# Perceiver and delta-rule block: inverses in whole lines, Gram halves by ScalarE with masks on GpSimd, new lists of turns

## The reference

```
x = x + xattn(layernorm(x), ctx)        # causal self-attention, attention over 257 context rows, FFN 128-512-128
x = x + attn(layernorm(x))              # two layers of a delta rule with 8 heads, each followed by a gated FFN of 352
x = x + ffn(layernorm(x))               # 32 experts of 64, top 8 within the best 4 of 8 groups, one shared expert
```

```
def step(S, inps):
    qi, ki, vi, bi = inps
    pred = jnp.einsum('bhkv,bhk->bhv', S, ki)
    S = S + bi[..., None, None] * ki[..., :, None] * (vi - pred)[..., None, :]
    o = jnp.einsum('bhkv,bhk->bhv', S, qi)
```

## Time and profile before

| what | value |
|---|---|
| median of three runs | 730.24 us (728.17 to 730.74) |
| the profiled execution | 727.0 us, of which the span is 725.2 |
| TensorE busy | 582.2 us, 80% |
| VectorE busy | 446.4 us, 62% |
| ScalarE busy | 269.7 us, 37% |
| GpSimd busy | 105.2 us, 15% |
| mean granted TensorE clock | 0.834 of full |

### The profile page before, as it was taken

One profiled execution on the slowest core, in us unless ns is written; L12 is line 12 of the kernel. 1 busy time (PEld: TensorE's weight loads), 2 busy tenths in 40 slices (PEclk: granted clock), 3 DMA queues, 4 the chain that ended last, 5 costly groups with the idle time before them and its releaser, 6 DMA issues.

```text
span 725.2 us, 15630 instructions
## 1 busy us (share of the span) xinstructions
PE 582.2 (80%) x6608; PEld 387.7 (53%) x6608; DVE 446.4 (62%) x1103; ACT 269.7 (37%) x571; POOL 105.2 (15%) x148
## 2 busy tenths in 40 slices
PE   2787970877598899787589768996688999999994
PEld 1543650466497867655388635873453444444442
DVE  4856495879947244937845881676666555555553
ACT  1465530554622634354544345234332222222221
POOL 2545372420000102110200010111200000000000
PEclk9888995775557599889657977898979999999998
DMA  9995013000000000000000220000122634334321
GB/s 343 309 368 208 1 23 95 0 2 3 1 3 4 1 3 2 2 1 2 0 2 4 85 103 2 3 3 1 34 61 64 147 87 118 100 101 117 87 59 29
DMA packets 19077, 46.68 MB, mean 64 GB/s; under 512 B 3808, under 2 KB 8544, under 8 KB 18752
## 3 DMA queue, kind: packets, MB, share of 16 engines
q1 hardware_dynamic: 18368, 45.43, 20.7%
q10 hardware_dynamic: 640, 0.26, 0.2%
HBM read 43.32 MB, written 2.36 MB: 63 GB/s over the span
## 4 chain that ended last, share of the span: by engine, by line
PE 60%; DVE 21%; ACT 9%; POOL 3%; SPq 2%; issue 2%; DMA 1%; DVEq 0%; POOLq 0%
PE psum L736 8%; PE psum L731 8%; PE psum L741 7%; PE psum L579 5%; ACT arena L759 4%; PE psum L606 4%; PE psum L668 3%; PE psum L694 3%; PE psum L565 3%; PE psum L697 3%; PE psum L703 2%; PE psum L657 2%; PE psum L647 2%; POOL rstd L939 2%; SPq L413 2%
## 5 line engine op out<-in xcount | busy, mean ns | idle before, releaser
L918 ACT ACTIVATE arena<-psum 128x512 f32<-128x512 f32 x68 | 40.6, 597 | 131.9 <-PE psum L731 124.0
L1358 DVE TENSOR_TENSOR arena<-psum,arena 128x512 f32<-128x512 f32 x64 | 44.3, 692 | 62.5 <-PE psum L736 60.7
L741 PE MATMUL psum<-arena,wed_sb 128*128 128x512 f32 x128 | 66.2, 599 | 0.0
L759 ACT ACTIVATE arena<-psum 128x512 f32<-128x512 f32 (+1 forms) x72 | 34.3, 503 | 63.9 <-PE psum L565 38.1
L565 PE MATMUL psum<-arena 32*64 32x128 f32 x1024 | 44.1, 331 | 11.5 <-DVE XA L1275 6.8
L1363 DVE TENSOR_TENSOR arena<-arena 128x512 f32<-128x512 f32 x64 | 44.3, 692 | 13.6 <-PE psum L741 13.6
L565 PEld LDWEIGHTS psum<-arena 32*64 32x64 f32 x1024 | 38.0, 167 | 17.9 <-DVE XA L1275 7.8
L938 POOL TENSOR_TENSOR ve<-ss,eps_rms 128x4 f32<-128x4 f32 x16 | 4.5, 282 | 291.9 <-ACT yr L810 208.1
L469 PE MATMUL psum<-ident,yn 128*128 128x128 f32 x72 | 15.9, 379 | 38.3 <-DVE yn L1024 21.3
L741 PEld LDWEIGHTS psum<-arena,wed_sb 128*128 128x128 f32 x128 | 24.9, 194 | 31.7 <-issue 24.0
L579 PE MATMUL psum<-wed_sb,arena 64*64 64x32 f32 x512 | 28.2, 291 | 14.7 <-ACT arena L759 14.7
(11 more groups left out here) (285 smaller groups left out, 1225.1 us busy)
## 6 DMA issues: line engine op xcount, KB each, us to landing
arena<-shares SPq DMA_DIRECT2D x64, 256.0 KB, 4.0
arena<-in_ctx_t SPq DMA_DIRECT2D x16, 514.0 KB, 8.6
arena<-in_ctx_z SPq DMA_DIRECT2D x16, 512.0 KB, 9.8
XA<-in_x SPq DMA_DIRECT2D x1, 1024.0 KB, 4.8
zlast<-in_ctx_last SPq DMA_DIRECT2D x4, 256.0 KB, 17.4
X<-x_mid SPq DMA_DIRECT2D x2, 512.0 KB, 4.4
weg_sb<-in_we_gate SPq DMA_DIRECT2D x2, 512.0 KB, 6.3
weu_sb<-in_we_up SPq DMA_DIRECT2D x2, 512.0 KB, 7.1
```

The lines of the kernel that those rows point to most:

```text
L741: pe.matmul(x3, wed_sb[:, (p - 1) % (NPAIR + 1), :], act_a[pr], start=(p == 0), stop=False, skip_group_check=True).then_inc(x_down[pr], 1)
L759: return act.activation(out_, in_, ACT.Copy, scale=scale)
L918: act.activation(act_g[pr], banks[4 * pr + 2 * (n % 2)], ACT.Silu).then_inc(x_silu[pr], 1)
L1358: dve.tensor_tensor(act_gu[pr], banks[4 * pr + 1], act_g[pr], ALU.mult).then_inc(x_gu[pr], 1)
```

## The change

There are four edits.

1. The transposed inverses are written to `back` with the 16 rows of a block side by side: `(n r)` in place of `(r n)`. VectorE's transpose back (L1306 after) so writes with a stride of 16 words, and the spread on ScalarE reads 16 words side by side.
2. ScalarE copies both halves of a Gram quarter, the key half to GA and the query half to BD, and signals after the second. TensorE's next quarter waits for that signal. The VectorE step is gone.
3. GpSimd multiplies each quarter of BD by the triangle in place, and signals `g_diag`; the "o" step on TensorE waits for the four of them.
4. Both lists of turns are other ones.

```diff
-XTURNS = "AABAABABBABAAAAAABABABABAABABBAABBBABBBABABBBB"
+XTURNS = "ABABAABBAABAAAAAABABABAABAABABBAABBBBBBABABBBB"
...
-TURNS = ("AABAABAABAABBAABABABAABBAABAABABBAABAABBAAAAAAABBABABAABBABABAABABABAABAABABABBBABABABABAABAABAB"
+TURNS = ("AAAABABABAABBBBBAAAAAABABABAABBABBAABABBABBAAAABAAAABBAABBABAAAAABBABAAAAAABBAAABABBAABAABBBABABB"
...
                         if q == 0:
                             pe.wait_ge(k_bq, i + 1)
                         else:
-                            pe.wait_ge(g_diag[u], pi * 4 + q)
+                            pe.wait_ge(g_a[u], pi * 4 + q)
...
                     elif kind == "o":
                         pe.wait_ge(s_u[u], pi * 3 + 3)
+                        pe.wait_ge(g_diag[u], pi * 4 + 4)
...
-                        copy(quarter(GA[g], q), gram_part(bank, 0)).then_inc(g_a[u], 1)
+                        copy(quarter(GA[g], q), gram_part(bank, 0))
+                        copy(quarter(BD[g], q), gram_part(bank, 1)).then_inc(g_a[u], 1)
...
-                        lanes = back[pr].rearrange("p (r n) -> p n r", r=C16)[:, u * NB:(u + 1) * NB, :]
+                        lanes = back[pr].rearrange("p (n r) -> p n r", r=C16)[:, u * NB:(u + 1) * NB, :]
...
+                    elif kind[:4] == "gram":
+                        q = int(kind[4])
+                        pool.wait_ge(g_a[u], (l * 2 + pr) * 4 + q + 1)
+                        pool.tensor_tensor(quarter(BD[g], q), quarter(BD[g], q),
+                                           bc(tril.unsqueeze(1).unsqueeze(1), [P, 4, 2, T]), ALU.mult).then_inc(g_diag[u], 1)
...
-                    elif kind[:4] == "gram":
-                        q = int(kind[4])
-                        dve.wait_ge(g_a[u], pi * 4 + q + 1)
-                        dve.tensor_tensor(quarter(BD[g], q), gram_part(bank, 1),
-                                          bc(tril.unsqueeze(1).unsqueeze(1), [P, 4, 2, T]), ALU.mult).then_inc(g_diag[u], 1)
...
-                            dve.transpose(back[pr], XL[pr]).then_inc(l_inv, 1)
+                            dve.transpose(back[pr].rearrange("p (n r) -> p r n", r=C16),
+                                          XL[pr].rearrange("p (r c) -> p r c", r=C16)).then_inc(l_inv, 1)
```

More of the change, by code:

```diff
@@ L86 @@
 ROUTE = ["eln", "etr", "elog", "ro0", "ro1", "ro2", "ec"]
-TURNS = ("AABAABAABAABBAABABABAABBAABAABABBAABAABBAAAAAAABBABABAABBABABAABABABAABAABABABBBABABABABAABAABAB"
-         "ABBABAAABBAABAABABABABABABABABABABABABAAABBBBBBBBBABAAABBABBABBBBBABABBBAABAAABAABABABBBABBAABBA"
-         "BBBABAABABBBAABABABAAABBBAABAABAABBBABABBBABBAABBBABAB")
+TURNS = ("AAAABABABAABBBBBAAAAAABABABAABBABBAABABBABBAAAABAAAABBAABBABAAAAABBABAAAAAABBAAABABBAABAABBBABABB"
+         "BAABBABAABABABBABAABABBBAAABABABAAAAABABABBBBABBABBABAABABABABABBBBBBAAABABAABBAABAABAABABABBABBB"
+         "BAABBBAAABBBAABBBBAAABABBBABAABABBAABBBABBABBBBABBBB")
 def cross_schedule():
```

## The result

The changed kernel takes 708.09 us in the median of four runs (705.14 to 723.41) against 730.49 for the kernel before on the same chip: a ratio of 0.968, interval 0.962 to 0.975. Two later measurements gave 0.963 [0.956, 0.970] and 0.969 [0.964, 0.974] (the square brackets hold 95% intervals). By the medians of all executions the three ratios are 0.969, 0.974 and 0.975. The rows compare with the profiled execution of before (727.0 us).

What follows compares the result with a forecast made beforehand. From 560 us TensorE never pauses at full clock; only earlier waits, VectorE and half-clock stretches could change. 727.0 + 5 - 2 - 6 = 724, plus 3.2 to the median, is 727 us; 8 in 10: 712 to 743.

Steps and rivals of the forecast that it cites:

- The cross part, +5: Before the layers: the new order makes the first context maximum 4 us late, 1 more charged; bounds +1 and +7.
- The masks' price: Layer 0's inverse: each GpSimd mask blocks a VectorE operation with two SBUF inputs for 1.05 us; seven hits, +7.4.
- the new way through the quarters: Layer 0, ahead of the extraction: four Gram quarters in a row at half clock, extraction at 167.5, no gain.
- Layers 0 and 1 behind the first spread, -3.6: Both layers after layer 0's first spread step: the -2 of parts 2 and 3, less TensorE's 1.6 late start there.
- the -2 of parts 2 and 3: Masks moved to GpSimd, and layer 1: together -2; bounds +9 (all masks hit) and -10 (none hit, full clock holds).
- The waits of the new list: Layer 0: A's feed-forward runs without B's steps between; p2, s3, p3 and n1 then wait, adding 4 to 6.
- The whole lines: Layer 0's spread: first four copies 2.8 us, not 4.3; transposes +0.6 each; layer 1's spread gives 2 to 3.
- The clock: Tail: less time at half clock, -1; layer 0's small tiles taken at half clock, by the row at 196 to 224.
- The rule on the clock that the prediction weighed: Layer 0's quarters: by the rule full clock and extraction some 5 us earlier; the prediction kept to the row, no gain.
- The tail, -6: From 480 to 560 us: A's routing and expert steps fill TensorE's waits in B's feed-forward; bounds -12 and 0.
- The faster rival: The lists fit and GpSimd's masks find gaps; layers -10, 717 us on the median (712 to 722); chance 0.27.
- The signs: Right if context maximum about 38.5, blocked operations 1.2 to 1.5, copies 0.71, no otr wait; slower if layer-1 extraction past 335.

Runs made afterwards that it cites:

- e16: Changed kernel with GpSimd's masks moved after the inverses at layer 0 only; ratio 0.956 [0.951, 0.961] against the kernel before.
- the execution of 723.4 us: Another profiled execution of the unaltered changed kernel: 723.4 us at a mean clock of 0.823.
- e14: Kernel before with only the whole lines added, under the old lists; 722.4 us against 729.5, ratio 0.988 [0.983, 0.992].
- e4: Kernel before with both new lists and none of the other edits; 743.7 us, ratio 1.011 [1.006, 1.015].
- e8: Changed kernel with the masks back on VectorE, whole lines and both new lists kept; ratio 0.987 [0.982, 0.992] against the kernel before, median 725.3 us.
- e1: Changed kernel run again unaltered for a profile; 708.95 us in the profile, six runs from 702.67 to 723.57 us.
- e10: Changed kernel with 55 filler matmuls ahead of the first spread of layer 0; ratio 0.982 [0.977, 0.987] against the kernel before.
- e2: Changed kernel with the old list of the cross part; one run 699.6 us, five 714.8 to 719.0 us.
- e12: Changed kernel with masks after the inverses at layer 0 and the old cross list; one run 691.3 us, five 705.8 to 707.2 us.

## Why the prediction was wrong, by its steps

**The cross part, +5: right.** A's p times V started at 21.27 us (21.6 was forecast), the first context maximum came at 39.0 (about 38.5), and TensorE was 5.0 us late at the end of the first projections (151.2 against 146.2), as charged.

**The masks' price: right in mechanism and near in size, the sum partly by luck.** GpSimd's masks took 1.30 to 1.41 us on average by tile (1.28 was taken), seven VectorE operations were blocked from the extraction on (6.2 us, 7.4 were charged), the copies out of the inverse took 0.71 (0.71 was taken), the transposes back 1.90. The first spread step began at 202.3; by the forecast it was 195.9 + 5 + 1.6 = 202.5. That it fits so closely is owed to two errors that cancel. A's own masks held the extraction up by 3.0 us, and the forecast had them at nearly nothing. Without them (e16) it starts at 169.96, only 2.6 later than before (167.37), although the cross part puts TensorE 5.0 behind; the new way through the quarters so gave some 2.4 us, for which the forecast said "no gain". e16 shows the price: without the blocks the kernel is 6.5 to 10 us faster. This agrees with the rule of the Trainium skill (SBUF — State Buffer, "Who interferes with whom") that the prediction set beside the row.

**Layers 0 and 1 behind the first spread, -3.6 (the -2 of parts 2 and 3, less the 1.6 above): wrong, -16.2.** This is the step that failed, and it has three mis-sized terms. The stretch of layer 0 gave -7.7 for a forecast of +0.4, that of layer 1 -8.5 for -4.

- *The waits of the new list.* A's feed-forward without B's steps between its own was charged with 4 to 6 us of waits. TensorE's idle time from the first spread to the end of A's projections fell from 6.7 to 2.4 us instead: the steps s3 and p3 of B that follow the feed-forward wait 0.41 and 0.16 us. The other 3.5 us of the -7.7 are a shorter busy time, and they are luck: in the execution of 723.4 us the same stretch is 96.2 us, 3.9 longer than before.
- *The whole lines.* They were priced as 1.5 us less for four copies, less 0.6 for the transpose, for each spread. e14 measured 9 us for all (6 to 12 by its interval). Cut at the same steps, its profile has TensorE idle for 2.0 us less behind the first spread of layer 0 and 5.9 less in layer 1, where the forecast gave the spread 2 to 3. In the new list they also shorten the wait ahead of A's spread of layer 1 (2.54 us in e4, 0.78 in e8), and with the short wait the spread is at full clock.
- *The clock.* "Less time at half clock, -1" stood in the tail, and nothing in the layers. The same matmuls took 17.0 us less. The forecast used the row at 196 to 224 us, where small matmuls run at 0.50 without a pause, as if small matmuls always did. It holds at the first spread of layer 0: 13.86 us for 256. It does not hold 34 us later (3.92 us for 128 in e1, 7.04 in the execution of 723.4 us), nor at A's spread of layer 1, where the stretch to s1 took 9.4 us in place of 16.6. These 7.2 us are in all three profiles of the changed kernel and are the largest single piece of the miss that belongs to the change.

How much of the gain is the clock's? Executions at like mean clocks give a rough answer: the kernel before took 729.2 us at 0.839 and 725.3 at 0.845; the changed one 718.2 at 0.839 and 713.5 at 0.850. That is 11 us at like clocks, as is the 11.6 us less idle time in the execution of 723.4 us. It is rough because a mean clock also counts the time in which TensorE is idle. The rest of the difference of 22 goes with mean clocks of 0.853 to 0.864, which the kernel before did not reach in any run (its highest is 0.847, at 724.8 us).

**The rule on the clock that the prediction weighed.** By the Trainium skill (TensorE: Matmul & The Clock Gate, Part 1) activity releases the throttle; the prediction set this against the row at 0.50, and held with the row. The runs bear out neither by itself. In e10 the clock was 0.86 from 185 to 200 us, with the 55 large matmuls, and 0.50 from 213.4 us on, though TensorE hardly paused. In e1 it was 0.50 from 202.3 to 236.1 us, busy for 33.3 of 33.8, and then rose to 1.00 with small matmuls before and behind and no wait between. The same row of small matmuls is so seen at either level, and the rise, where it comes, comes in the midst of it.

**The tail, -6: right in sign and in the bounds, -8.3.** The waits for n2 and etr went further down than forecast (0.80 and 2.02 us are left of 6.87 and 4.88, where 2.1 and 3.5 were expected), and a wait of 3.36 us came up at 513.84, of the kind that was charged with 2.5 for B's fin. What was not seen are the stores of the result: 2.8 us by having A's issued while B still computes.

**The sum.** The forecast's terms, cut at the same steps, are +6.6, -3.6 and -6, together -3; measured were +6.4, -16.2 and -8.3, together -18.1. The faster rival had the right sign and the wrong reason: it assumed that the masks would find gaps, and at layer 0 they did not. The -10 that it gave the layers came (-9.8), but through shorter waits elsewhere and the clock. The signs behaved as for the forecast: operations of 1.2 to 1.4 us beside the masks, copies of 0.71, no wait at either "otr" of layer 0, and the extraction of layer 1 at 321.7 us (335.94 before, about 327 forecast).

**What stays open.** What sets the level of the clock: a short wait goes with full clock at A's spread of layer 1 in all profiles, but e10 has 0.40 us of waiting and half clock behind it, and at A's "o" of layer 0 the level differs between executions with the same instructions ahead. Why the low times are rare with the old cross list (e2, e12) is open too, and so is whether some order reaches them always. Of the Gram edits, ScalarE's copies without GpSimd's masks were not run apart.

## What to carry to other kernels

When a list of turns and an edit to the engines come together, price them together: here the new lists alone lose 1.1%, all the edits alone gain 0.4%, and together they gain 3.1%. For the list the reason is shown: it waits for a result that the edit brings forward (e4). For the edits it is not: under the old lists the masks come with a first spread that is 4.1 us later and no gain to pay for it. Only the whole lines pay by themselves (1.2%). Work moved to GpSimd should run where VectorE reads PSUM or is idle; here the same 16 masks cost 6.5 to 10 us beside the inverse, and behind it, from 210 to 230 us in e16, they took 1.24 us each and no VectorE operation beside them was longer than usual. Where the mean clock of a stretch lies between the two levels, widen the forecast's range by it and not only by waits: of the 18.1 us between two executions here 17.0 were the busy time of the same matmuls. And look at more than one execution before a level is called the work of the change: here one stretch is at full clock in every profile, another in some only.

## What the runs showed that was not expected

- The mean granted clock of executions of one unchanged kernel went from 0.819 to 0.864, and its times from 702.7 to 723.6 us.
- The clock can fall within a nearly unbroken row of small matmuls: after 55 large ones, 64 small took 2.06 us, and the next 192 took 10.45, with 0.40 us of waiting between. It can also rise within one: from 0.50 to 1.00 at 236.8 us of e1, with no wait there.
- A ScalarE copy of 128x512 that read one word in each 256 bytes took 1.18 us, one that reads runs of 64 bytes took 0.71, while the VectorE transpose that has to scatter for it went from 1.25 to 1.90.
